# Third attention part: three of its closing products placed elsewhere in the order

## The chip, the cores and the metric

The kernel runs on one core of one Trainium2 chip. The metric is the device time in microseconds (us) of one execution. A core has five engines that each take their own list of instructions strictly in turn: TensorE (PE, matrix products; PEld are its weight loads), VectorE (DVE), ScalarE (ACT), GpSimd (POOL) and SyncE (SP, which here issues DMAs). They wait for one another by semaphores. TensorE writes only to PSUM, eight banks of 128 partitions by 512 fp32 numbers; VectorE and ScalarE carry results from there to SBUF.

## What is computed

Four decoder layers, each with a self-attention, a cross part and a feed-forward part, on x of shape (4, 512, 128), in fp32. The change is in the self-attention of the third layer (in the code `attn2`), causal, with 16 heads of 8 numbers and a learned vector for each clipped distance:

```python
q, k = rotary(shape(x @ w_q.T)), rotary(shape(x @ w_k.T))     # (B, 16, 512, 8)
q = q / sqrt(8)
rel = rel_emb[clip(pos[None, :] - pos[:, None], -32, 32) + 32]
scores = einsum('bhqd,bhkd->bhqk', q, k) + einsum('bhqd,qkd->bhqk', q, rel)
scores = where(causal, scores, NEG_INF)
attn = softmax(scores, axis=-1)
ctx = einsum('bhqk,bhkd->bhqd', attn, v) + einsum('bhqk,qkd->bhqd', attn, rel)
x = x + ctx.transpose(0, 2, 1, 3).reshape(B, L, 128) @ w_o.T
```

## The kernel before, in words

The program is a row of stages; all engines finish one before the next begins. The third attention part is class `Attention2` (line 1356) on top of `Attention` (line 1083), with the distance terms in `Near` (line 1571). It works through batches b of 0 to 3, query tiles of 128 rows (qt, 0 to 3), groups of four heads (g, 0 to 3) and heads j within the group: 4 x 4 x 4 x 4 = 256 units. A unit of query tile qt spans the (qt + 1) x 128 keys up to the diagonal.

What a unit needs, and on which engine:
- *scores*: PE multiplies the masked queries with the keys (`ps<-parts`, one row of 128x128 up to 128x512), DVE reduces the far keys to a minimum (L337) and adds the distance term to the last 160 keys with a running minimum (L343).
- *exp*: ACT takes the exponential from PSUM (L318) and sums it.
- *turned*: four units later PE transposes the weights tile by tile (L311, `ps<-wc_sb,fw_sb 128x128`), and ACT and DVE in turn copy them out of PSUM (L317, L334).
- *inverse*: once in a group DVE takes the reciprocals of four sums (L358); POOL packs the near weights with them (L328) and SP sends them through DRAM to skew them.
- *values*: once in a group PE multiplies the turned weights with the values (L307, `ps<-fw_sb,work` or `ps<-fw_sb`, x8 to x32 in a row).

When the fourth group of a query tile has its values, the *ending* of that tile starts. Its steps, in order:
1. *out*: ACT copies the values' bank (128x512) to SBUF, and DVE spreads the sixteen reciprocals to 512 columns (L334, `fw_sb<-work` or `fw_sb<-fw_sb`, 128x512).
2. *wide*: PE turns that spread table by four products with the identity (L307, `ps<-wc_sb,fw_sb 128x128` x4 in the program; each appears as two in the trace, so x8).
3. *scaled*: DVE multiplies the copied values with it (L321, `fw_sb<-fw_sb,ps`).
4. *output*: PE multiplies with w_o (L307, `ps<-fw_sb,wr_sb 128x128` x4, x8 in the trace).
5. *added*: DVE adds that to x (L321, `xT_sb<-xT_sb,ps`).
6. *weights*, *near values*, *near output* (`Near.ending`, line 1591): PE transposes the skewed near weights (L311, `ps<-wc_sb,work`), DVE copies them (L334, `work<-ps`), PE multiplies with the distance vectors (L307, `ps<-work 128x128` x4), ACT copies, PE multiplies with w_o (L307, `ps<-work,wr_sb`), DVE adds to x.

The order of all this is a list, `self.order`, that `Attention.plan` (line 1118) writes while the kernel is built; every engine then walks the same list and emits what is its own. `step()` is called once after each unit and advances each generator in `bg` to its next `yield`: one is `ending`, another `prepare` (line 1374), which makes the next batch's operands during query tile 3 and places the near product (step *near*) at the start of each query tile. A `yield` is thus one unit's distance. The near product of a tile goes out to DRAM by SP, comes back skewed, and the first scores of that tile wait for it on DVE.

All products other than scores, turned and values share two PSUM banks, ps[6] and ps[7] (`Banks`, line 395): each takes the next bank in turn that is not held, and PE waits in `free` (line 1199) until the bank's last user has been read. *wide* holds its bank until *scaled*, *output* until *added*:

```python
    shared = {"wide": "scaled", "output": "added"}
```

PE's *wide* also waits for the spread table of the DVE, and DVE's *scaled* for *wide*.

Of the kernel before, what the change touches and what calls it, by code (L numbers as in the profile page):

```python
# [1082 lines left out]
class Attention(Stage):  # L1083
# [99 lines left out]
    def ending(self, br):  # L1183
        o = self.order
        self.O.take(br)
        o.append(("out", br))
        yield
        o.append(("wide", br))
        yield
        o.append(("scaled", br))  # L1190
        yield
        yield
        o.append(("output", br))
        yield
        o.append(("added", br))
        if self.rel is not None:
            yield from self.rel.ending(self, br)
# [373 lines left out]
class Near:  # L1571
# [18 lines left out]

    def ending(self, a, br):
        self.PS.take(br)
        for _ in range(7):
            yield
        for what in ("weights", "near values", "near output"):
            a.order.append((what, br))
            yield
            yield

# [2183 lines left out]
```

How the kernel before makes its waits and increments, by code:

```python
    def wait_ge(self, sem, v):  # L301
        if self.e is not None and self.seen.get(sem.name, 0) < v:
            self.e.wait_ge(sem, v)
            self.seen[sem.name] = v
# [282 lines left out]
    def sums_pe(self, e, c):  # L587
        k, t = self.k, self.tag
        e.wait_ge(*k.made_a[t, "square", c])
        e.wait_ge(*k.made_a[t, "deviation", c - 2])
        for i in range(4):
            ins = e.matmul(self.sums[c][:, 64 * i:64 * i + 64], self.sq[:, tile(4 * c + i)], k.cst("mean")[:, 0:64])
        ins.then_inc(*k.summed.up((t, "variance", c)))
# [1 line left out]
    def spread_pe(self, e, c):  # L595
        k, t = self.k, self.tag
        e.wait_ge(*k.made_v[t, "root", c])
        e.wait_ge(*k.made_v[t, "normed", c - 2])
        for i in range(4):
            ins = e.matmul(self.spread[c][:, tile(i)], view(self.r[:, 4 * c + i:4 * c + i + 1], [0, 128]), k.cst("id"))
        ins.then_inc(*k.summed.up((t, "spread", c)))
# [8 lines left out]
    def square_act(self, e, c):  # L610
        k, t = self.k, self.tag
        e.wait_ge(*k.summed[t, "centred", c])
        e.activation(self.sq[:, ch(c)], k.ps[c][:, :], ACT.Square).then_inc(*k.made_a.up((t, "square", c)))
# [1 line left out]
    def root_act(self, e, c, eps):  # L615
        k, t = self.k, self.tag
        e.wait_ge(*k.summed[t, "variance", c])
        e.activation(self.r[:, 4 * c:4 * c + 4], view(self.sums[c], [64, 4]), ACT.Sqrt, bias=k.cst(eps)
                     ).then_inc(*k.made_a.up((t, "deviation", c)))
# [1401 lines left out]
    def turned_pe(self, e, i, X):  # L2021
        e.wait_ge(*self.k.made_a[self.tag, "out", i])
        for c in range(4):
```

## Time and profile before

| | |
|---|---|
| time, median of 3 runs | 3057.36 us (3053.97 to 3064.7) |
| the profiled execution: its time | 3065.82 us |
| the profiled execution: its span | 3064.0 us |
| its mean granted TensorE clock | 0.926 |
| busy over the span | PE 89%, PEld 50%, DVE 56%, ACT 40%, POOL 38% |
| the stage of the change | from 1494 to 1912 us, 418 us |

Times are from one execution taken by the profiler. The granted clock is the share of TensorE's full speed that it was given; matrix products overlap, so that a busy PE is not a PE at its peak. "Idle before" is how long the engine had nothing to do before a row, with the engine that ended the wait.

### The profile page before, as it was taken

The page shows a single profiled execution, that of the slowest core. Times are in us where ns is not written, and L with a number is a line of the kernel's source. Part 1 is how long each engine was busy: PE and PEld are TensorE (multiplying, and loading weights), DVE is VectorE, ACT ScalarE, POOL GpSimd, SP SyncE. Part 2 cuts the span into 40 slices and gives each one's busy share as a digit, 9 for nine tenths or more (in the row PEclk, how much of TensorE's full clock was granted, in tenths as well). Part 3 has the DMA queues.
Part 4 walks back from the last instruction along what each step waited for, and adds up shares of the span by engine and source line. Part 5 has one row for each costly group of instructions (what it writes and reads, how often), then busy time and mean ns, then how long its engine had stood idle before and what let it go on. Part 6 is the DMA issues. An engine that isn't in the chain of part 4 may idle for free. (4 is left out here: it accounts for less than half of the span.)

```text
span 3064.0 us, 39617 instructions
## 1 busy us (share of the span) xinstructions
PE 2734.3 (89%) x15416; PEld 1543.3 (50%) x15416; DVE 1700.6 (56%) x2993; ACT 1223.9 (40%) x2546; POOL 1149.6 (38%) x1045
## 2 busy tenths in 40 slices
PE   6999998899989998978788888999979898998899
PEld 2544454646654444446456656566533333334556
DVE  3444443533337882259587777356466676765623
ACT  1233232333325663133355555366533343432422
POOL 2322220265541100042445443099524443442265
PEclk8999998899997999889799999899989999998999
DMA  2000001011110002046212222211000000001032
GB/s 93 1 1 1 1 1 73 1 56 55 42 53 1 1 1 88 32 101 182 73 54 75 70 58 56 95 42 52 4 1 1 1 1 1 1 1 47 1 132 104
DMA packets 33566, 126.47 MB, mean 41 GB/s; under 512 B 8929, under 2 KB 11746, under 8 KB 27202
## 3 DMA queue, kind: packets, MB, share of 16 engines
q1 hardware_dynamic: 31842, 120.79, 12.1%
q0 software_dynamic: 1536, 3.15, 0.4%
q8 instruction: 121, 1.98, 0.3%
q14 instruction: 67, 0.55, 0.1%
HBM read 106.86 MB, written 17.06 MB: 40 GB/s over the span
## 5 line engine op out<-in xcount | busy, mean ns | idle before, releaser
L307 PE MATMUL ps<-parts 128*128 128x512 f32 (+8 forms) x5544 | 1211.5, 433 | 87.5 <-DVE fw_sb L337 39.7
L307 PEld LDWEIGHTS ps<-parts 128*128 128x128 f32 (+3 forms) x5544 | 673.7, 191 | 610.3 <-issue 291.1
L317 ACT ACTIVATE work<-ps 128x512 f32<-128x512 f32 (+5 forms) x954 | 520.8, 571 | 955.9 <-PE ps L307 862.0
L321 POOL TENSOR_TENSOR work<-work 128x512 f32<-128x512 f32 x380 | 508.3, 1353 | 502.3 <-ACT work L317 298.4
L337 DVE TENSOR_REDUCE fw_sb<-ps 128x2 f32<-128x1024 f32 (+3 forms) x384 | 415.4, 1087 | 274.3 <-PE ps L307 273.3
L307 PE MATMUL ps<-work 128*32 128x256 f32 (+5 forms) x2396 | 365.5, 422 | 8.5 <-DVE work L334 4.9
L307 PE MATMUL ps<-work,fw_sb 128*128 128x512 f32 (+1 forms) x720 | 327.5, 554 | 13.7 <-DVE work L321 8.2
L317 ACT ACTIVATE fw_sb<-ps 128x512 f32<-128x512 f32 (+5 forms) x394 | 204.8, 537 | 308.0 <-PE ps L307 263.9
L321 DVE TENSOR_TENSOR work<-work,ps 128x512 f32<-128x512 f32 (+1 forms) x196 | 121.9, 622 | 283.1 <-POOL work L321 273.0
L311 PE MATMUL ps<-wc_sb,fw_sb 128*128 128x128 f32 x1128 | 209.2, 299 | 36.5 <-DVE work L358 11.7
L307 PEld LDWEIGHTS ps<-work 128*32 128x32 f32 (+2 forms) x2396 | 139.3, 138 | 170.1 <-issue 135.8
L311 PEld LDWEIGHTS ps<-wc_sb,fw_sb 128*128 128x128 f32 x1128 | 133.5, 148 | 104.1 <-issue 28.5
L307 PE MATMUL ps<-fw_sb,wr_sb 64*128 64x512 f32 (+3 forms) x452 | 176.0, 650 | 10.8 <-DVE fw_sb L321 5.3
L318 ACT ACTIVATE fw_sb<-ps,work 128x128 f32<-128x128 f32 (+3 forms) x256 | 135.1, 528 | 118.5 <-DVE work L343 95.2
L321 POOL TENSOR_TENSOR fw_sb<-fw_sb 128x512 f32<-128x512 f32 (+1 forms) x63 | 114.1, 1812 | 166.2 <-ACT fw_sb L317 97.3
L307 PEld LDWEIGHTS ps<-work,fw_sb 128*128 128x128 f32 x720 | 131.6, 197 | 75.6 <-issue 26.0
L317 ACT ACTIVATE work<-ps,wr_sb 128x512 f32<-128x512 f32 (+1 forms) x159 | 108.4, 682 | 129.1 <-PE ps L307 128.9
L334 POOL COPY fw_sb<-work 128x512 f32<-128x512 f32 x32 | 19.6, 611 | 328.7 <-DVE work L358 328.7
L321 POOL TENSOR_TENSOR fw_sb<-fw_sb,work 128x1024 f32<-128x1024 f32 x44 | 103.9, 2360 | 70.4 <-ACT work L317 70.4
L343 DVE CUSTOM_DVE_ANT_0 ps<-ps,work 128x160 f32<-128x160 f32 (+1 forms) x256 | 116.2, 460 | 20.6 <-PE ps L307 10.0
L307 PE MATMUL ps<-fw_sb,work 128*32 128x128 f32 (+3 forms) x1316 | 125.6, 354 | 1.8 <-DVE fw_sb L334 1.6
L328 POOL TENSOR_SCALAR wr_sb<-fw_sb,work 128x160 f32<-128x160 f32 (+1 forms) x176 | 78.1, 527 | 124.5 <-DVE work L358 119.1
(141 smaller groups left out, 3121.9 us busy)
## 6 DMA issues: line engine op xcount, KB each, us to landing
work<-scr_w SPq DMA_DIRECT2D x29, 1024.0 KB, 4.7
work<-scr_places SPq DMA_DIRECT2D x64, 256.0 KB, 4.0
work<-scr_sk SPq DMA_DIRECT2D x64, 128.0 KB, 2.7
scr_sp<-wr_sb SPq DMA_DIRECT2D x64, 128.0 KB, 2.2
fw_sb<-in_f SPq DMA_DIRECT2D x1, 6528.0 KB, 19.3
fw_sb<-in_f SPq DMA_DIRECT2D x1, 5376.0 KB, 15.1
fw_sb<-in_f SPq DMA_DIRECT2D x1, 4608.0 KB, 18.0
work<-scr_w SPq DMA_DIRECT2D x8, 512.0 KB, 5.7
```

What stands on the lines that cost most here:

```text
L307: return self.e.matmul(o, l, r, start=start, stop=stop) if self.e else Unwritten()
L311: return self.e.transpose(o, i, identity[0:n, 0:n]) if self.e else Unwritten()
L317: return self.e.activation(o, i, f, bias=bias, scale=scale)
L318: return self.e.activation(o, i, f, bias=bias, scale=scale, accum_out=accum)
L321: return self.e.tensor_tensor(o, a, b, op) if self.e else Unwritten()
L328: return self.e.tensor_scalar(o, a, s1, s2, op0, op1)
L334: return self.e.tensor_copy(o, i) if self.e else Unwritten()
L337: return self.e.tensor_reduce(o, i, AX.X, op, negate=neg) if self.e else Unwritten()
L343: return self.e.tensor_tensor_reduce(o, a, b, 1.0, low, ALU.add, ALU.min, accum)
```

## The change

```diff
...
         self.O.take(br)
         o.append(("out", br))
-        yield
+        for _ in range(3):
+            yield
         o.append(("wide", br))
         yield
         o.append(("scaled", br))
-        yield
-        yield
+        for _ in range(4):
+            yield
         o.append(("output", br))
         yield
         o.append(("added", br))
...
         self.PS.take(br)
-        for _ in range(7):
-            yield
+        yield
+        yield
         for what in ("weights", "near values", "near output"):
             a.order.append((what, br))
             yield
             yield
+            yield
```

The first two hunks are in `Attention.ending`, the last in `Near.ending`. Counted in calls of `step()` behind *out* (the first comes after the exp of the unit in which *out* stands), the steps of an ending stand before and after at: *wide* 1 and 3, *scaled* 2 and 4, *output* 4 and 8, *added* 5 and 9, *weights* 12 and 11, *near values* 14 and 14, *near output* 16 and 17. No instruction is added or taken away, and the banks are dealt out anew, since they go by the order. `Attention` has no other subclass, so no other stage changes.

PE, batch 0, at the ending of query tile 1, which falls into the second group of tile 2 (`ps<-parts` is a unit's scores, x8 of 32x128 the values, x3 of L311 a unit's transposes, `wc_sb,fw_sb 128x128 x4` is *wide*, `work,wr_sb` *near output* of the tile before). Before:

```order
L307 MATMUL ps<-work,wr_sb 128x128
L307 MATMUL ps<-parts 128x384
L307 MATMUL ps<-fw_sb,work 32x128 x8
L311 MATMUL ps<-wc_sb,fw_sb 128x128 x3
L307 MATMUL ps<-wc_sb,fw_sb 128x128 x4
L307 MATMUL ps<-parts 128x384
L311 MATMUL ps<-wc_sb,fw_sb 128x128 x3
L307 MATMUL ps<-parts 128x384
L311 MATMUL ps<-wc_sb,fw_sb 128x128 x3
```

and after:

```order
L307 MATMUL ps<-parts 128x384
L307 MATMUL ps<-fw_sb,work 32x128 x8
L311 MATMUL ps<-wc_sb,fw_sb 128x128 x3
L307 MATMUL ps<-work,wr_sb 128x128
L307 MATMUL ps<-parts 128x384
L311 MATMUL ps<-wc_sb,fw_sb 128x128 x3
L307 MATMUL ps<-parts 128x384
L311 MATMUL ps<-wc_sb,fw_sb 128x128 x3
L307 MATMUL ps<-wc_sb,fw_sb 128x128 x4
L307 MATMUL ps<-parts 128x384
```

*wide* moved behind the scores and transposes of two more units, and *near output* from ahead of the values to behind the transposes that follow them.

PE, batch 0, at the ending of query tile 2, which falls into the second group of tile 3 (`lnT_sb,wr_sb 128x512` is a product of `prepare`: the first here *turn*, the second *sine*, of the next batch's queries). Before:

```order
L307 MATMUL ps<-work,wr_sb 128x128
L307 MATMUL ps<-lnT_sb,wr_sb 128x512
L307 MATMUL ps<-parts 128x512
L307 MATMUL ps<-fw_sb,work 32x128 x12
L311 MATMUL ps<-wc_sb,fw_sb 128x128 x4
L307 MATMUL ps<-lnT_sb,wr_sb 128x512
L307 MATMUL ps<-wc_sb,fw_sb 128x128 x4
L307 MATMUL ps<-parts 128x512
L311 MATMUL ps<-wc_sb,fw_sb 128x128 x4
```

and after:

```order
L307 MATMUL ps<-lnT_sb,wr_sb 128x512
L307 MATMUL ps<-parts 128x512
L307 MATMUL ps<-fw_sb,work 32x128 x12
L311 MATMUL ps<-wc_sb,fw_sb 128x128 x4
L307 MATMUL ps<-work,wr_sb 128x128
L307 MATMUL ps<-lnT_sb,wr_sb 128x512
L307 MATMUL ps<-parts 128x512
L311 MATMUL ps<-wc_sb,fw_sb 128x128 x4
```

*wide* left this place; *near output* now stands between the two products of `prepare`. By the dealing of banks, *sine* stood in the bank that *near output* had left and *wide* in that of *turn*; now *sine* stands in the bank of *turn*.

PE, in the same tile, from the last products of *value* (`wr_sb,wc_sb`) on (`parts 128x512` are scores and, in front of other scores, *stack*, the next batch's keys; `fw_sb,wr_sb` is *output*). Before:

```order
L307 MATMUL ps<-wr_sb,wc_sb 128x128
L307 MATMUL ps<-parts 128x512
L311 MATMUL ps<-wc_sb,fw_sb 128x128 x4
L307 MATMUL ps<-parts 128x512 x2
L307 MATMUL ps<-fw_sb,wr_sb 128x128 x4
L307 MATMUL ps<-parts 128x512
L307 MATMUL ps<-fw_sb,work 32x128 x16
L311 MATMUL ps<-wc_sb,fw_sb 128x128 x4
L307 MATMUL ps<-parts 128x512 x3
```

and after:

```order
L307 MATMUL ps<-wr_sb,wc_sb 128x128
L307 MATMUL ps<-wc_sb,fw_sb 128x128 x4
L307 MATMUL ps<-parts 128x512
L311 MATMUL ps<-wc_sb,fw_sb 128x128 x4
L307 MATMUL ps<-parts 128x512 x3
L307 MATMUL ps<-fw_sb,work 32x128 x16
L311 MATMUL ps<-wc_sb,fw_sb 128x128 x4
L307 MATMUL ps<-parts 128x512 x3
```

*wide* now follows *value* directly, ahead of the next scores, and *output* has left this place: it stands four units later, one unit ahead of the next batch's near product. The second *stack* product used the bank of the first; now it uses the bank of *wide*.

## Rows read from the trace of the kernel before

**Rows 1.** Stage window: us, busy PE, PEld, DVE, ACT, POOL (instructions), clock, DMA.
```profile
1494.00:1912.00 418.00, 345.13 (x2842) 247.05 (x2841) 314.37 (x1042) 218.87 (x689) 198.92 (x349) 0.91 0.23 64
```

**Rows 2.** Waits in the stage: who waited for whom, us in all, times, longest.
```profile
ACT fw_sb L318 <- DVE work L343: 95.2, 134, 2.9
...
DVE work L337 <- PE ps L307: 28.8, 18, 2.7
```

**Rows 3.** Timeline behind query tile 1 of batch 1: start, us, [idle before].
```profile
1651.56 0.64 PE L307 MATMUL ps<-fw_sb 128*32 128x128 f32 x16
...
1653.53 0.53 DVE L334 COPY fw_sb<-fw_sb 128x512 f32<-128x512 f32 x1
...
1654.12 2.08 PE L307 MATMUL ps<-wc_sb,fw_sb 128*128 128x128 f32 x8 [1.44 <-DVE fw_sb L334]
...
1656.55 0.39 DVE L337 TENSOR_REDUCE work<-ps 128x1 f32<-128x224 f32 x1 [2.03 <-PE ps L307]
```

**Rows 4.** Groups of L337 in the stage: busy, mean ns, idle before.
```profile
L337 DVE TENSOR_REDUCE work<-ps 128x1 f32<-128x96 f32 x64 | 15.7, 245 | 6.1 <-PE ps L307 6.1
...
L337 DVE TENSOR_REDUCE work<-ps 128x1 f32<-128x224 f32 x64 | 24.2, 379 | 7.0 <-PE ps L307 7.0
...
L337 DVE TENSOR_REDUCE work<-ps 128x1 f32<-128x352 f32 x64 | 33.0, 515 | 15.8 <-PE ps L307 15.7
```

**Rows 5.** Timeline of VectorE behind query tile 2 of batch 3.
```profile
1884.61 0.53 DVE L337 TENSOR_REDUCE work<-ps 128x1 f32<-128x352 f32 x1 [0.88 <-PE ps L307]
```

**Rows 6.** Timeline in query tile 2 of batch 1, behind its first groups.
```profile
1658.12 1.16 PE L307 MATMUL ps<-fw_sb,wr_sb 128*128 128x128 f32 x8
...
1661.50 0.44 PE L307 MATMUL ps<-parts 128*128 128x384 f32 x1 [0.23 <-ACT fw_sb L318]
...
1662.91 0.39 DVE L337 TENSOR_REDUCE work<-ps 128x1 f32<-128x224 f32 x1
```

**Rows 7.** Timeline in query tile 3 of batch 1.
```profile
1681.84 1.16 PE L307 MATMUL ps<-wc_sb,fw_sb 128*128 128x128 f32 x8 [1.59 <-DVE work L331]
...
1683.27 0.53 DVE L337 TENSOR_REDUCE work<-ps 128x1 f32<-128x352 f32 x1 [1.49 <-PE ps L307]
...
1684.98 0.49 PE L307 MATMUL ps<-wr_sb,lnT_sb 128*128 128x128 f32 x2 [0.64 <-DVE work L331]
...
1690.96 1.91 PE L307 MATMUL ps<-fw_sb,wr_sb 128*128 128x128 f32 x8
...
1693.33 0.52 DVE L337 TENSOR_REDUCE work<-ps 128x1 f32<-128x352 f32 x1 [2.73 <-PE ps L307]
...
1696.93 0.97 PE L307 MATMUL ps<-parts 128*128 128x512 f32 x3 [1.38 <-DVE parts L334]
...
1697.93 0.53 DVE L337 TENSOR_REDUCE work<-ps 128x1 f32<-128x352 f32 x1 [0.87 <-PE ps L307]
```

**Rows 8.** Timeline from the near product of batch 1 to its first scores.
```profile
1602.17 0.69 DVE L334 COPY work<-ps 128x512 f32<-128x512 f32 x1 [0.17 <-PE ps L307]
...
1602.89 1.70 SPq L372 DMA_DIRECT2D scr_sk<-work  x4
...
1610.76 0.38 DVE L343 CUSTOM_DVE_ANT_0 ps<-ps,work 128x128 f32<-128x128 f32 x1 [2.27 <-DMA work<-scr_sk]
```

**Rows 9.** Timeline in query tile 0 of batch 1.
```profile
1616.97 1.06 PE L307 MATMUL ps<-wc_sb,fw_sb 128*128 128x128 f32 x8
...
1618.12 0.38 DVE L343 CUSTOM_DVE_ANT_0 ps<-ps,work 128x128 f32<-128x128 f32 x1 [0.67 <-PE ps L307]
```

**Rows 10.** Timeline at the stage's end.
```profile
1904.93 1.70 SPq L372 DMA_DIRECT2D work<-scr_sp  x4
...
1908.44 0.66 PE L311 MATMUL ps<-wc_sb,work 128*128 128x128 f32 x4 [0.58 <-DVE xT_sb L321]
```

**Rows 11.** Windows behind one ending, and in query tile 3, of batch 1.
```profile
1652.00:1656.00 4.00, 2.56 (x20) 2.19 (x12) 2.45 (x9) 1.72 (x5) 2.95 (x5) 0.71 0.43 112
...
1688.00:1692.00 4.00, 4.00 (x15) 3.40 (x15) 1.95 (x5) 1.34 (x4) 1.81 (x4) 0.50 0.00 0
```

## The prediction

> **What bounds the kernel now.** The order is written out by hand, so I read the stage alone. First its window: PE is busy for 345.1 of 418 us and DVE for 314.4, at a granted clock of 0.91 [rows 1]. Neither is full, so waits decide, and I went to them. Two stand out: ACT waits for DVE's running minimum, 95.2 us in 134 waits, each short, and DVE waits for PE ahead of its reduction L337, 28.8 us in only 18 waits [rows 2]. The first says that in the ordinary run of units DVE leads and the others follow. The second is time in which this leader stands, in few large pieces, and that is what a change of the order can give back.
>
> Where the pieces are, the timeline tells. Behind query tile 1 of batch 1, PE has done the values and the transposes, and the next thing in its list is *wide*. DVE spreads the reciprocals only at 1653.53, so PE stands for 1.44 us, then takes 2.08 us for *wide*, and the scores behind it come late: DVE's next reduction starts after 2.03 us of idle [rows 3]. The groups by form sort the 28.8 us by query tile, since the width of L337 does: 6.1 us in tile 1, 7.0 in tile 2, 15.7 in tile 3 [rows 4]. In tiles 1 and 2 the waits are one for each of the four batches, all behind *wide*. In tile 3 they are four waits behind *wide* (1.49 us at the batches 0 to 2, as in the first DVE row of rows 7, and 0.88 at batch 3 [rows 5]), and six others, 15.7 - 3 x 1.49 - 0.88 = 10.3 us, all in batches 0 to 2, where the next batch is prepared.
>
> **The change part by part.** No instruction comes or goes; only waits can change.
>
> *Wide* two units later, in tiles 1 and 2, and in tile 3 of batch 3 (nine places). PE goes on with the next scores, while DVE spreads the reciprocals and turns to its next unit; when PE reaches *wide*, the table is two units old. The stall goes whole: 6.1 + 7.0 + 0.9 = 14.0 us. What is late next? *Wide* itself still takes 1.1 us of PE, ahead of a unit's scores. The cover is the pair of scores that PE has in hand. In rows 6 the scores product at 1661.50 had waited 0.23 us for ACT and is read by DVE at 1662.91, so it is finished about 1.0 us early (1662.91 less 1661.94). A block of 1.16 us ahead of it eats first the wait and then 0.9 of this 1.0. The trace has the case: *output*, 1.16 us at 1658.12, stands in the same kind of place, and no wait of DVE follows it [rows 6]. I take nothing for *wide* and for *output* at the new places. Bounds: 14.0 us gained, and from that down by up to 1.16 us at each of nine *wides* (10.4) if the cover is missing.
>
> *Wide* in tile 3 of batches 0 to 2 (three places). Here PE's stall of 1.59 us ended with a DVE instruction of L331, not with the spread table [rows 7]: *wide* stood in the bank of *turn*, and had to wait until DVE had read it. After the change *sine* stands in that bank, right in front of the same scores, and waits for the same read. It is a product of 1.0 us like *wide*. So the 3 x 1.49 = 4.5 us stay. Bounds: nothing to 4.5 us gained.
>
> The Trainium skill, "Perfetto Trace Analysis", section "Matmuls", says that independent groups of products should rotate through the PSUM banks, so that the read-out of one overlaps the next. By that rule the new *turn* and *sine* in one bank speak against the change, and the three stalls of 1.49 us stay. The trace agrees as far as it goes: the 1.59 us are a wait for a bank's reader [rows 7].
>
> The rest of tile 3, batches 0 to 2. (a) *Wide* now follows *value*. *Value* itself no longer waits 0.64 us for its bank [rows 7], *wide* adds 1.06: the next scores come 0.4 us later. (b) *Output* leaves its place at 1690.96, where it held PE until 1692.52 (the next row starts there), 1.56 us, and DVE stood 2.73 [rows 7]: 1.6 us gained; *scaled*, 0.68 us of DVE, falls into the idle time that is left there. (c) The second *stack* has another bank than the first, so that PE's 1.38 and DVE's 0.87 us [rows 7] go: 0.9 gained. (d) *Output* now stands one unit ahead of the near product of the next batch. DVE copies it at 1602.17 after waiting 0.17 for PE, and then 8.6 us of DRAM and back pass until the first scores of the next batch, which wait 2.27 us for that transfer [rows 8]. Whatever delays the copy, delays the batch: 1.0 us lost for an *output* at full clock. Sum: -0.4 + 1.6 + 0.9 - 1.0 = 1.1, I take 1.0 us for each batch, 3.0 in all. Bounds: all six waits gone, 10.3 us gained; and, with both products at the 1.9 us that *output* took here [rows 7] and nothing but (b) and (c) returned, 0.64 - 1.9 + 1.6 + 0.9 - 1.9 = -0.7 a batch, 2.0 us lost.
>
> The endings of tile 3, which fall into tile 0 of the next batch (three). *Wide* follows PE's own work without a wait there, and DVE stands 0.67 us after it [rows 9]: in these short units PE leads. The same 1.06 us come two units later. Nothing; bounds one wait each, 3 x 0.67 = 2.0 us either way.
>
> *Weights* one unit earlier, *near output* one later: the transposes wait for the transfer of the packed weights, which at the stage's end is issued at 1904.93 and waited for no longer than 1908.44 [rows 10], 3.5 us; and PE stands behind no DMA there: its wait of 0.58 us is for DVE. Nothing. SP's list keeps its order. In the tail *weights* of the last tile start 0.04 us after DVE's addition but also just when the transfer is in, so a shorter chain has nothing behind it: nothing, to 0.5 either way.
>
> Sum: 14.0 + 0 + 3.0 = 17.0 us. Against the profiled execution, 3065.8, whose span is 3064.0, that makes 3048.8. That execution lies 8.5 us above the median of the runs, 3057.36, and above their highest, 3064.7; I take the same microseconds off the median: 3057.4 - 17.0 = 3040.4 us.
>
> **The rivals.**
>
> A. *The clock comes back too.* In the 4 us around the stall of rows 3 the granted clock was 0.71, and where tile 3's *output* ran it was 0.50, the lower level of 1.2 GHz, with PE busy all of the 4 us and DVE 1.95 of them [rows 11]. Take the stalls away and PE may keep 2.4 GHz; then also the six waits of tile 3 and the stall in front of *sine* shrink. For it: the 1.91 us of *output* against 1.16 elsewhere. Against it: the stall of 1.59 us that precedes the low stretch stays. All 28.8 us go: 3057.4 - 28.8 = 3028.6. The skill's page "TensorE: Matmul & The Clock Gate", section "A second HAM failure mode: psum-queue depth-cycling", describes short idles between groups of products that make the clock swing between its levels; by it, this is how it goes.
>
> B. *The products show again.* *Wide* at the end of a group comes when DVE has just waited for the reciprocals' sums and the cover is thin; DVE waits 0.6 us at each of the twelve places in tiles 1 to 3 (1.06 of *wide* and 0.44 of scores, less a cover of 0.9), and tile 3 goes by its lower bound. For it: the cover of rows 6 is just long enough. Against: *output* there. 14.0 - 7.2 - 2.0 = 4.8 us gained: 3052.6, which a measurement of this kernel can't tell from no change.
>
> C. *Slower: PE falls to the lower clock for longer.* A mean of 0.91 [rows 1], if all of it is time at half speed, is 0.18 x 418 = 75 us at the lower level. In such a stretch DVE stands for 2.05 of 4 us [rows 11], half of the time. Of the stage's 103.6 us of DVE idle (418 - 314.4 [rows 1]) that is 38, and the other 66 spread over 343 us, 0.19 of the time. Each microsecond more at the lower level thus costs 0.32. If *value* with *wide*, and *output* with the values behind it, leave gaps in which the clock falls, and the low time doubles, 75 x 0.32 = 24 us are lost: 3057.4 - 14.0 + 24 = 3067.4. It decides from some 72 more us at 1.2 GHz ((14.0 + 9.2) / 0.32). Against it: the change removes idle time of PE.
>
> **How the numbers follow.** My forecast 0.61, with a range of its own of 3034 to 3047 (17.0 us, from 23 down to 10); A 0.14, B 0.16, C 0.09. This kernel's measurement can tell some 0.3%, 9.2 us, from no change: faster is below 3048.2, slower above 3066.5. Faster: 0.59 of the forecast and A, 0.73. Slower: C, 0.08. The same: B and the rest, 0.19. The range must reach from near A to past B: 3030 to 3055, leaving out C and half of A.
>
> **What would show it.** Right: the wait of L337 for PE falls from 28.8 to some 12 us, and its parts for 96 and 224 columns to nearly nothing; the four products of *wide* have no idle before them in tiles 1 and 2; in tile 3 *sine* of the queries has 1.1 us or more of idle, ended by DVE L331, and the 1.49 us of DVE behind it stay; no 1.38 us in front of the second *stack*. The copy of the near product waits about 1 us for PE, and the first scores of batches 1 to 3 still wait for the transfer. Wrong: a stage that is not 10 us shorter than 418, DVE waits of 0.5 us or more behind the new *wide* or *output* (B), or a stage clock under 0.88 (C) or over 0.95 (A).

## The result, and the profile after

| | before | after |
|---|---|---|
| median of five runs each, side by side | 3053.97 us (3052.38 to 3064.7) | 3036.34 us (3034.98 to 3042.4) |
| ratio, with its 95% interval | | 0.9939 (0.9919 to 0.9959) |
| the same kernel in a later session, 29 and 12 runs | 3052.04 us (3039.46 to 3069.63) | 3043.46 us (3032.54 to 3055.61) |
| ratio there | | 0.9959 (0.9938 to 0.9980) |
| span and granted clock of the profiled execution | 3064.0 us, 0.926 | 3033.4 us, 0.935 |

By the ratios the change gains 18.6 us (12.5 to 24.7) in the first session and 12.5 us (6 to 19) in the second; by the medians it is 17.6 and 8.6. 17.0 were predicted.

The window of the stage, cut at the same points of the work as in [rows 1] (columns as there), and two of its parts, query tile 3 of batch 1 and of batch 2:

```profile
1486.80:1892.10 405.30, 332.22 (x2842) 239.70 (x2840) 314.91 (x1042) 217.75 (x689) 198.77 (x349) 0.93 0.23 66
1656.39:1691.48 35.09, 27.60 (x248) 20.21 (x247) 29.83 (x76) 18.06 (x44) 12.71 (x22) 1.00 0.13 31
1752.32:1793.56 41.24, 33.70 (x248) 24.80 (x247) 30.03 (x77) 17.84 (x44) 12.68 (x22) 0.83 0.10 26
```

12.7 us are gone from 418.00. VectorE works as long as before (314.91 us), so what went is its idle time. The last two rows are the same instructions in the same order, and one takes 6 us more than the other, at a granted clock of 0.83 against 1.00. That must be kept in mind for all of tile 3.

The wait behind the 28.8 us of [rows 2], and the groups of L337 that answer to [rows 4]:

```profile
DVE work L337 <- PE ps L307: 10.3, 12, 1.7
DVE parts L334 <- PE ps L307: 9.7, 6, 2.2
```

```profile
L337 DVE TENSOR_REDUCE work<-ps 128x1 f32<-128x352 f32 x64 | 33.0, 516 | 9.3 <-PE ps L307 9.2
...
L337 DVE TENSOR_REDUCE work<-ps 128x1 f32<-128x224 f32 x64 | 24.3, 379 | 0.0
...
L337 DVE TENSOR_REDUCE work<-ps 128x1 f32<-128x96 f32 x64 | 15.8, 247 | 1.1 <-PE ps L307 1.1
```

The 7.0 us of tile 2 are 0.0, the 6.1 of tile 1 are 1.1 (all in batch 1, at a clock of 0.91), the 15.7 of tile 3 are 9.2. The second wait was 4.9 us in three waits before. What is new is VectorE's copy of the *stack* products at the turn from one batch to the next, 4.7 us in three waits.

A part of what went in tile 2 belongs to the clock. Tile 2 of batches 0 and 1 of the kernel before, of batch 1 of the changed kernel, and of batch 0 of e10 (a later run, with *wide* at its new place; columns as in [rows 1]):

```profile
1544.56:1566.97 22.41, 19.11 (x178) 13.43 (x176) 19.43 (x66) 14.23 (x43) 11.20 (x20) 1.00 0.26 72
1645.82:1669.34 23.52, 19.88 (x175) 14.42 (x173) 19.49 (x66) 14.12 (x43) 11.19 (x20) 0.93 0.25 69
...
1634.86:1656.39 21.53, 18.30 (x178) 13.16 (x177) 19.52 (x66) 14.10 (x43) 11.18 (x20) 1.00 0.28 75
...
1539.44:1560.84 21.40, 19.16 (x178) 14.25 (x177) 19.38 (x67) 14.32 (x43) 11.19 (x20) 0.92 0.28 75
```

At full clock the tile went from 22.41 to 21.53 us, 0.9 less. At the old place a low clock costs 1.0 us more, since *wide* itself then takes 2.0 to 2.1 us in place of 1.16 while VectorE stands for it; three of the four tiles 2 of the profile before were such. At the new place a low clock costs nothing in this tile (21.40 at 0.92); in tile 1 of batch 1, where it met *wide* too, it still cost 1.1 us.

The ending of query tile 1 of batch 1, answering to [rows 3]:

```profile
1642.37 0.66 DVE L334 COPY fw_sb<-fw_sb 128x512 f32<-128x512 f32 x1
...
1643.61 0.38 DVE L337 TENSOR_REDUCE work<-ps 128x1 f32<-128x224 f32 x1
...
1643.93 1.06 PE L307 MATMUL ps<-wc_sb,fw_sb 128*128 128x128 f32 x8
...
1644.43 0.38 DVE L337 TENSOR_REDUCE work<-ps 128x1 f32<-128x224 f32 x1
```

The table is spread 0.9 us before *wide* begins, TensorE takes *wide* without idle time, and VectorE's reductions on either side don't wait.

Query tile 3 of batch 1, answering to [rows 7], and the same place in batch 2 from its *value* on:

```profile
1668.36 0.68 DVE L331 SCALAR_TENSOR_TENSOR work<-ps,wr_sb 128x512 f32<-128x512 f32 x1
1669.09 1.13 PE L307 MATMUL ps<-lnT_sb,wr_sb 128*128 128x512 f32 x2 [2.99 <-DVE work L331]
...
1670.48 0.52 DVE L337 TENSOR_REDUCE work<-ps 128x1 f32<-128x352 f32 x1 [1.45 <-PE ps L307]
...
1773.89 2.08 PE L307 MATMUL ps<-wc_sb,fw_sb 128*128 128x128 f32 x8
1774.00 0.69 DVE L334 COPY fw_sb<-ps 128x512 f32<-128x512 f32 x1 [3.18 <-PE ps L307]
...
1776.43 0.53 DVE L337 TENSOR_REDUCE work<-ps 128x1 f32<-128x352 f32 x1 [1.74 <-PE ps L307]
```

*Sine* waits for the reader of *turn*, 2.99 us, and VectorE then stands 1.45. In batch 2 TensorE fell to half clock behind that, *wide* took 2.08 us, and VectorE stood 3.18 and 1.74 us more, which batch 1 did not.

The turn from batch 0 to batch 1, answering to [rows 8]:

```profile
1590.73 0.69 DVE L334 COPY work<-ps 128x512 f32<-128x512 f32 x1 [0.17 <-PE ps L307]
...
1595.85 3.13 PE L307 MATMUL ps<-parts 128*128 128x512 f32 x6 [2.90 <-DVE parts L334]
...
1597.96 0.69 DVE L334 CAST parts<-ps 128x512 fp32r<-128x512 f32 x1 [2.17 <-PE ps L307]
...
1600.10 0.38 DVE L343 CUSTOM_DVE_ANT_0 ps<-ps,work 128x128 f32<-128x128 f32 x1 [1.45 <-PE ps L307]
...
1602.02 0.69 DVE L334 COPY work<-ps 128x512 f32<-128x512 f32 x1 [1.49 <-PE ps L307]
```

The near copy waits 0.17 us, as before. The first scores of the batch wait no longer for the transfer but for TensorE, which is in the chain of stack products and their copies. TensorE stood 2.90 us in front of the second of them and was at half clock from 1.2 to 4.6 us behind the tile's start, while it made this one and the next two.

### The profile page after: what moved, and what is told of

Same layout as the page of the kernel before. It is cut to its first block and busy times, and to the rows that moved or that the text cites. A ratio compares the mean times of both kernels' runs of the same rounds, so it can differ in the third digit from the quotient of the medians.

```text
span 3033.4 us, 39609 instructions
## 1 busy us (share of the span) xinstructions
PE 2703.9 (89%) x15416; PEld 1528.3 (50%) x15416; DVE 1700.5 (56%) x2993; ACT 1221.4 (40%) x2546; POOL 1149.9 (38%) x1045
## 5 line engine op out<-in xcount | busy, mean ns | idle before, releaser
L337 DVE TENSOR_REDUCE fw_sb<-ps 128x2 f32<-128x1024 f32 (+3 forms) x384 | 415.3, 1087 | 269.3 <-PE ps L307 268.3
L311 PE MATMUL ps<-wc_sb,fw_sb 128*128 128x128 f32 x1128 | 207.8, 297 | 48.3 <-DVE fw_sb L334 15.4
L311 PEld LDWEIGHTS ps<-wc_sb,fw_sb 128*128 128x128 f32 x1128 | 132.5, 146 | 116.4 <-issue 30.3
L307 PE MATMUL ps<-fw_sb,wr_sb 64*128 64x512 f32 (+3 forms) x452 | 169.4, 626 | 10.7 <-DVE fw_sb L321 4.9
L321 DVE TENSOR_TENSOR parts<-work,parts 128x512 fp32r<-128x512 f32 x68 | 80.7, 1191 | 77.4 <-ACT parts L317 77.4
## 6 DMA issues: line engine op xcount, KB each, us to landing
fw_sb<-in_f SPq DMA_DIRECT2D x1, 4608.0 KB, 17.6
```

Of the source, the lines that this page charges most:

```text
L307: return self.e.matmul(o, l, r, start=start, stop=stop) if self.e else Unwritten()
L311: return self.e.transpose(o, i, identity[0:n, 0:n]) if self.e else Unwritten()
L321: return self.e.tensor_tensor(o, a, b, op) if self.e else Unwritten()
L337: return self.e.tensor_reduce(o, i, AX.X, op, negate=neg) if self.e else Unwritten()
```

## The experiments

Each kernel's stage is split here by query tile, from one tile's last reciprocals (L358) to the next one's: us in tile 1, in tile 2 (four each), in tile 3 of batches 0 to 2 with the granted clock of each, and in tile 0 of batches 1 to 3. The total has the two remaining tiles too, tile 0 of batch 0 and tile 3 of batch 3. Times and ratios are against the kernel before of the same session; three sessions, in the order of the numbers 1 to 4, 5 to 8, 9 to 12.

| kernel | tile 1 | tile 2 | tile 3, b0-2 | clock there | tile 0, b1-3 | total | median us | ratio (95%) |
|---|---|---|---|---|---|---|---|---|
| before | 80.8 | 92.7 | 114.6 | .91 .91 .95 | 60.5 | 385.7 | 3053.4, 3052.0, 3049.7 | 1 |
| after | 74.9 | 86.1 | 113.0 | .95 1.00 .83 | 62.5 | 372.8 | 3036.3 | .9939 |
| e5 after again | 74.7 | 86.1 | 111.8 | 1.00 .91 .91 | 62.7 | 371.6 | 3043.5 | .9959 (.9938-.9980) |
| e1 wide only | 75.1 | 85.5 | 117.1 | .91 .87 .87 | 62.2 | 375.9 | 3041.2 | .9973 (.9955-.9991) |
| e2 near only | 78.5 | 91.5 | 115.0 | .87 1.00 .96 | 63.7 | 385.7 | 3053.3 | 1.0004 (.9985-1.0022) |
| e3 output only | 79.7 | 90.6 | 112.5 | .91 .91 .95 | 62.5 | 382.2 | 3047.5 | .9997 (.9977-1.0016) |
| e4 near output 16 | 75.3 | 85.5 | 101.2 | 1.00 .90 1.00 | 63.2 | 361.2 | 3029.4 | .9932 (.9907-.9957) |
| e6 after, wide x2 | 76.1 | 86.1 | 114.4 | .91 .95 .95 | 65.3 | 378.1 | 3045.1 | .9977 (.9953-1.0000) |
| e7 before, wide x2 | 85.6 | 94.7 | 112.5 | .95 1.00 .96 | 65.2 | 396.4 | 3068.0 | 1.0034 (1.0016-1.0052) |
| e8 e4 + stack earlier | 73.3 | 85.4 | 98.7 | 1.00 1.00 1.00 | 58.0 | 351.4 | 3019.1 | .9878 (.9847-.9908) |
| e9 after, idle filled | 73.8 | 86.1 | 114.3 | .96 .96 .96 | 63.0 | 372.6 | 3040.4 | .9966 (.9946-.9985) |
| e10 e4 + stack by two | 73.9 | 85.4 | 102.8 | 1.00 1.00 1.00 | 63.7 | 361.9 | 3031.6 | .9922 (.9897-.9946) |
| e11 after, wide x4 | 83.0 | 93.0 | 127.4 | .92 .88 .84 | 70.9 | 412.0 | 3077.2 | 1.0082 (1.0050-1.0114) |
| e12 before, stack earlier | 83.0 | 90.7 | 113.0 | .91 .95 .95 | 66.4 | 390.1 | 3056.9 | 1.0012 (.9994-1.0030) |

**e1, e2, e3: one part at a time.** Steps behind *out* of *wide*, *scaled*, *output*, *added*, *weights*, *near values*, *near output*:

```diff
-before  1 2 4 5 12 14 16
+e1      3 4 6 7 12 14 16
+e2      1 2 4 5 11 14 17
+e3      1 2 8 9 12 14 16
```

> Only wide (and scaled behind it) moves, from 1 unit behind out to 3; output goes from 4 to 6 to stay behind scaled, weights, near values and near output stay at 12, 14 and 16. Theory (the gain is the removed wait of TensorE for the spread table): the stalls in tiles 1 and 2 go (12.5 us by the trace of the changed kernel), and in tile 3 of batches 0 to 2 sine of the queries stands in the bank that near output left one unit earlier, not in that of turn, so the three stalls of 1.45 us go as well: 14 to 20 us below the kernel before, thus level with the changed kernel or up to 4 us better. L337's wait for TensorE: 5 to 9 us. Rival (the gain comes from the three products together, by a higher clock): at most 8 us below before, and the stage's clock no higher than before.

> Only the near steps move: weights 12 to 11, near output 16 to 17; wide and output stay. Theory: nothing in tiles 1 and 2 (the 12.5 us of stalls stay); in tile 3 of batches 0 to 2 the bank of turn goes to sine instead of wide, so the 1.49 us only change place; in tile 0 of batches 1 and 2 the near product's copy loses about 1.0 us each by the new bank order. Time 0 to 3 us above the kernel before. Rival (the near steps carry a part of the gain): 3 us or more below.

> Only output moves, from 4 to 8 units behind out. Theory: tiles 1 and 2 as before (output is covered at both places), tile 3 of batches 0 to 2 gains 1.6 us each where output left the stack products and loses up to 1.0 at the near product: 0 to 3 us below the kernel before; L337's wait for TensorE 22 to 28 us. Rival (output's place sets the clock of tile 3): tile 3 of batches 0 to 2 gains 3 us each, 9 us in all.

Moving *wide* alone brings the whole gain of tiles 1 and 2 (13.0 us of it in the profile), and the times of e2 and e3 can't be told from before. How large the gain is depends on the clock of the profile that it is measured against: with *wide* at its old place tiles 1 and 2 took 173.5 us in before and 173.7 in e12, but 170.0 in e2 and 170.3 in e3, and with *wide* alone moved 160.5. So it lies between 9.5 and 13 us. *Output* at 8 (e3) takes 0.7 us off each tile 3, at the same clocks as before.

But e1 missed its expectation: 8 us by the ratio (3 to 14) and 12 by the medians, not 14 to 20, and L337 waited 17.4 us for TensorE, not 5 to 9. Tile 3 lost 2.5 us, although *sine* no longer waited for *turn*. TensorE in tile 3 of batch 0 of e1, and VectorE behind it:

```profile
1581.54 2.07 PE L307 MATMUL ps<-fw_sb,wr_sb 128*128 128x128 f32 x8 [1.57 <-ACT parts L317]
...
1584.08 0.52 DVE L337 TENSOR_REDUCE work<-ps 128x1 f32<-128x352 f32 x1 [3.89 <-PE ps L307]
```

At 6, *output* stands in the bank of the second *stack* and waits for ScalarE to have copied it, 1.6 us in each of the three batches. At 8 it does not. So e1 exchanges one stall for another. That it is worse than the changed kernel is not shown: its tile 3 of batch 0 takes 38.15 us at a clock of 0.91, and e5 has 38.31 at the same clock; its two longer tiles had 0.87, and the ratios of e1, after and e5 overlap.

**e4: *near output* back at 16.** The changed kernel with the last step one unit earlier, 3 4 8 9 11 14 16.

> The changed kernel with near output back at 16 units, so that it again stands ahead of turn of the queries and sine gets the bank that near output left. Theory (the idle before sine is the reader of its bank): the idle of TensorE before sine of the queries (2.99 us in batch 2) and the 1.45 us of VectorE behind it go in three places, and the near product of tile 1 again gets the bank of near values, which gives back the 1.0 us in tile 0 of batches 1 and 2: 4 to 6 us below the changed kernel, 22 to 25 below the kernel before. Rival (sine waits because VectorE is late with everything there, or the stall moves on to value, whose bank is now that of turn): within 1.5 us of the changed kernel.

Tile 3 of batch 0, where *sine* now has the bank that *near output* left:

```profile
1565.03 1.12 PE L307 MATMUL ps<-lnT_sb,wr_sb 128*128 128x512 f32 x2 [0.29 <-DVE xT_sb L321]
...
1566.43 0.68 DVE L334 COPY fw_sb<-ps 128x512 f32<-128x512 f32 x1
1567.03 0.67 DVE L331 SCALAR_TENSOR_TENSOR work<-ps,wr_sb 128x512 f32<-128x512 f32 x1
1567.63 0.51 DVE L337 TENSOR_REDUCE work<-ps 128x1 f32<-128x352 f32 x1
```

2.99 us of TensorE have become 0.29, and VectorE doesn't stand. The tile takes 32.72 us at a clock of 1.00, where the changed kernel takes 35.09 and 35.11 at 1.00; at about 0.91 it is 35.79 against 38.31. So the other deal of banks is worth 2.4 us a tile, not the 1.45 of the stall's one row: the wait of 0.57 us behind *value* and *wide* is gone too. And the clock stayed at 1.00 in two of three.

```profile
1555.25:1587.97 32.72, 28.02 (x248) 20.13 (x247) 29.50 (x76) 18.09 (x44) 12.78 (x22) 1.00 0.13 33
```

Tile 3 lost 10.6 to 11.8 us against the two profiles of the changed kernel, twice the 4 to 6 us that were expected of the whole kernel; tile 0 gave nothing back (63.2), so that part of the expectation was wrong. The times don't resolve e4 from the changed kernel: 0.9932 against 0.9939 and 0.9959, with intervals that overlap.

**e5: the changed kernel again.**

> The changed kernel once more, for a second profile and for its spread. Theory (query tile 3 of batches 0 to 2 is the same in its first 18 us, and then the granted clock falls or does not, by no order of its own): each of these three tiles takes some 35 us where the clock stays at 1.00 and 36.5 to 41 where it falls, in other batches than in the first profile; tiles 1 and 2 repeat within 0.3 us; time 3032 to 3045. Rival (the clock in a tile belongs to the order): 36.7, 35.1 and 41.2 us for batches 0, 1 and 2 again.

The low clock came in other batches: 35.1, 38.3 and 38.4 us, where the first profile had 36.7, 35.1 and 41.2. Tile 2 repeated to 0.02 us, tile 1 of batches 0 and 1 differed by 0.6 and 0.8, at another clock.

```profile
1561.72:1596.83 35.11, 27.58 (x248) 20.18 (x247) 29.87 (x77) 18.09 (x44) 12.76 (x22) 1.00 0.11 31
1657.99:1696.30 38.31, 30.77 (x248) 22.53 (x247) 30.05 (x77) 17.86 (x44) 12.74 (x22) 0.91 0.11 29
```

**e6, e7, e11: how much work the places cover.**

```diff
-                for c in range(4):
-                    ins = e.matmul(X[:, tile(c)], self.wide[:, tile(c)], k.cst("id"))
+                for c in range(8):
+                    ins = e.matmul(X[:, tile(c % 4)], self.wide[:, tile(c % 4)], k.cst("id"))
```

> The changed kernel with the four products of wide issued twice into the same bank: 1.06 us more of TensorE at each of 16 places. Theory (the new place is covered by about 1.0 us in tiles 1 and 2, so one wide is hidden and a second is not): 0.5 to 1.0 us at each of the eight places in tiles 1 and 2, 0.3 to 1.0 in tile 3 and 0: 6 to 14 us above the changed kernel. Rival 1 (there is ample cover): under 3 us in tiles 1 and 2 together. Rival 2 (the first wide already shows): the full 1.06 us at each, 17 us.

> The kernel before with the products of wide issued twice. Theory (TensorE stands for the spread table and VectorE then stands for TensorE, so every bit of work added there shows): 1.06 us or more at each of the eight places in tiles 1 and 2, and in tile 3: 12 to 18 us above the kernel before. Rival (wide was hidden there too, and only the table's lateness counted): under 6 us.

> The changed kernel with the four products of wide issued four times: 3.2 us more of TensorE at each of 16 places. With two times, tiles 1 and 2 took no more than 0.1 us each more at a clock of 1.00. Theory (the cover at the new place is about 2 us, since TensorE's idle time in the two units around counts beside the scores finished early): 1 to 2 us at each of the eight places in tiles 1 and 2, 8 to 16 us there. Rival (there is slack for 3 us and more): under 4 us in these eight tiles. In tile 3 and tile 0 about 2.5 us more each in both.

At the new place a second *wide* costs next to nothing in tiles 1 and 2, as the first rival of e6 had it and not its theory: -0.1 us in all of tile 2, and 1.3 in tile 1 against e5, 1.8 of it in batch 3 alone, where the clock was 0.92 and not 1.00. At the old place it costs 6.8 us in these eight tiles, 0.85 of its 1.06 each (tile 2 at full clock goes from 22.41 to 23.27); of the whole kernel it costs 10 us by the ratio (5 to 16) and 16 by the medians, where 12 to 18 were expected. Four times *wide*, 3.2 us more at each place, costs 8.3 in tile 1 and 6.9 in tile 2, 1.9 a place, within the 8 to 16 us expected; in tile 3 it costs 15.6 us, twice what was expected, at lower clocks than in e5, and in tile 0 8.2. The cover in tiles 1 and 2, the first *wide* included, is thus 4.2 - 1.9 = 2.3 us (an estimate from these runs), where 0.9 to 1.0 were read from the trace. VectorE behind a doubled *wide* (TensorE has it from 1651.69 to 1653.64) in e6:

```profile
1652.88 0.55 DVE L334 COPY fw_sb<-ps 128x384 f32<-128x384 f32 x1
1653.76 0.18 DVE L358 RECIPROCAL work<-work 128x4 f32<-128x4 f32 x1 [0.33 <-ACT fw_sb L318]
1653.86 0.39 DVE L337 TENSOR_REDUCE work<-ps 128x1 f32<-128x224 f32 x1
```

Between the two reductions it has a copy and the reciprocals, and waits there for ScalarE; the scores that *wide* delays come just in time. In tiles 3 and 0, without such room, e6 pays.

**e9: the idle time filled.** In *near output* of the tiles that fall into tile 3, ahead of its own wait:

```diff
+        if qt == 1 and b < 3:
+            for _ in range(4):
+                e.matmul(X[:, :], k.wt(2, "wk"), k.lnT[:, ch(b)])
```

> The changed kernel, with four products of 128x512 (some 1.8 us of TensorE, their result is overwritten) put ahead of near output in query tile 3 of batches 0 to 2. They fall into the 2.99 us in which TensorE stands in front of sine, of which 1.1 us remain; VectorE's 1.45 us and its waits stay as they are. Theory (the granted clock falls because TensorE has just stood idle for about 3 us): the clock of tile 3 stays near 1.00 in batches 0 to 2 and each of them takes 35 to 36 us, where the changed kernel had 35.1, 35.1, 36.7, 38.3, 38.4 and 41.2: 3 to 8 us below the changed kernel. Rival (the dip comes from something else, or more work makes the clock fall more): tile 3 at a clock of 0.83 to 0.95 in at least two of three, and no time below the changed kernel.

The four products took 3.60 us, not 1.8, so *near output* came late and VectorE stood 1.33 us more for it: the run prices the filling badly. TensorE then stood 1.0 us in front of *sine*, not 3.0. The clock still tells something. In the 5 us behind the start of *sine* it had fallen in 8 of the 12 profiled tiles with the whole stall (after, e5, e6, e11) and in none of the 9 without (e4, e8, e10), and here it stayed at 1.00 in all three. With the other profiles it is 10 of 15 (e2 has the stall too) against 1 of 24 (before, e1, e3, e7, e12 don't have it there). The limit of 5 us is arbitrary, and near it the counts are soft: one tile of e4, one of e1 and two of e6 fell 5.2 to 5.5 us behind that start. In e9 it fell in all three tiles at 6.2 to 6.3 us, where *value* ends and *wide* runs, with TensorE busy from *sine* on, and the tile had 0.96 in the mean. So neither expectation was met: the counts speak for a part of the idle time in the early fall, and what makes the later one is open.

**e8, e10, e12: the turn of a batch.** In `prepare`, behind the near product of the next batch; e8 and e12 take away one yield (e8 on top of e4, e12 on the kernel before), e10 both on top of e4:

```diff
             self.rel.plan(self, b, 0)
             yield
-            yield
             self.Q.take(b)
```

> Near output at 16 as in the earlier run, and the first stack product of the next batch's queries one unit earlier (one yield less behind the near product), so that the last unit of a batch holds one step less of the chain stack, copy, stack between TensorE and VectorE. Theory (at the turn of a batch this chain ends last, no longer the near transfer): 1 to 1.5 us less at each of three turns, 3 to 4.5 us below the version with near output at 16, 3022 to 3028. Rival (the near transfer, 8.6 us from its copy to the scores, is hardly earlier than the chain): 0 to 1 us less.

> As the version with near output at 16 and the first stack of the queries one unit earlier, but two units earlier, right behind the near product. Theory (the chain stack, copy, stack bounds the turn of a batch): another 0.5 to 1.3 us at each of three turns, until the near transfer ends last: 1 to 4 us below that version. Rival (the near transfer already ends last, and stack 0 now stands in the near product's own bank and ahead of its copy's turn in the order): 0 to 3 us above it.

> The kernel before, with only the first stack product of the next batch's queries one unit earlier. Theory (before, the first scores of a batch waited for the near transfer, 2.27 us, so that the chain of stacks was hidden): 0 to 1.5 us below the kernel before in all. Rival (the chain of stacks ended last before as well): 3.5 to 5 us below it.

e8 is the best kernel found: 1.2% below before by the ratio, and 24.4 us below the changed kernel of its session. Its profile has 5.2 us less than e4 in tile 0 (58.0 against 63.2), where 3 to 4.5 were expected of the whole kernel; at a like clock (0.91 and 0.92) it is 1.3 to 1.4 us a turn. It has the full clock in all three tiles 3, and L337 hardly waits any more:

```profile
DVE work L337 <- PE ps L307: 1.4, 3, 0.5
```

One step more (e10) loses it again, more than either of its expectations had: tile 3 takes 34.3 us in place of 32.9, at full clock in both, and the near product of the next tile is then copied only after VectorE has stood for 3.60 us in tile 0 of batch 1, and the clock there is 0.84 in all three.

```profile
1603.23 0.69 DVE L334 COPY work<-ps 128x512 f32<-128x512 f32 x1 [3.60 <-PE ps L307]
```

On the kernel before (e12) the same edit gives nothing, at most 1.8 us by the ratio, which excludes the rival's 3.5 to 5; in the profile tile 0 is 5.9 us longer: *weights* stand in another bank, the first scores wait 3.13 us for TensorE, and the clock is 0.85 to 0.89 there. What an edit at the turn is worth thus depends on the order that it is made in.

## Why the prediction was right, by its steps

- *Wide* in tiles 1 and 2 and at the end: 14.0 us predicted. Measured 5.9 + 6.6 + 0.8 = 13.3 in the first profile, 6.1 + 6.6 + 0.8 = 13.4 in the second. Right in place, and e1 shows that *wide* alone carries it. The size has some luck in it: both the 14.0 and the 13.3 are measured against one profile, in which the stalled *wide* took 1.59 to 2.08 us in six of the eight tiles 1 and 2, where it takes 1.16 at full clock. In tile 2, 3.5 of the 6.6 us are the stall at full clock, and 3.1 are what the low clock added to it. Against e2 and e3, with *wide* at its old place as well, tiles 1 and 2 gained 9 us.
- The cover of the new place: right that it holds, too small by more than half (2.3 us in place of 1.0). It was read off one product finished early; the copy, the reciprocals and their wait that VectorE also has in these units were not counted. Rival B hung on the cover being thin: e6 shows that in tiles 1 and 2 twice the work would hardly have shown.
- The stall moves from *wide* to *sine* in tile 3 of batches 0 to 2: the row is there in all three batches, 1.45 us where 1.49 was said. That nothing is gained there was right. Its price was not: e4 shows 2.4 us a tile for the bank that *sine* stands in.
- The rest of tile 3: 3.0 us predicted with no part for the clock. All of this tile, batches 0 to 2, gained 1.7 and 2.8 us in the two profiles. That these are near the sum is partly luck, for the tile's duration goes from 35.1 to 41.2 us with the clock. At like clocks the gain is smaller: 38.71 us before against 38.31 and 38.38 at 0.91, 37.20 against 36.65 at 0.95, thus 0.3 to 0.6 a tile where 1.0 was said. The waits of (b) and (c), 2.73 and 0.87 us, are gone as predicted, so the sum of the terms is about twice too large; which of them is mis-sized, these runs don't tell. Term (d) as put is refuted: the near copy waits 0.17 us, not 1.0.
- The endings in tile 0: nothing predicted, 2.0 and 2.2 us lost, at the edge of the bounds. The failed step is that the first scores of a batch wait for the near transfer; before, they did so in batches 1 and 2 and waited for TensorE in batch 3, where its clock was low. With the new order of the banks the second *stack* of the queries waits for the copy of the first (before, it had the near product's bank), *weights* stand ahead of it, and the chain of TensorE and VectorE ends last. e8 shortens this chain and gets 5.2 us. How much of the 2.0 is the chain and how much the clock is open: before, the two turns at full clock took 19.8 us and the one at 0.88 took 21.0, and the changed kernel has 20.8 to 21.0 at 0.92 in all six.
- Tail and *near output*: nothing predicted; from the last reciprocals to the last addition 12.9 us before and after.
- The sum: 17.0 predicted, 12.9 and 14.1 us in the stage's two profiles, 18.6 and 12.5 in the two sessions. The profiled spans differ by 30.6 us, and 17.7 of that lie outside the stage, where nothing was changed: the profiled execution of before was among its slowest, as the prediction had allowed for by counting from the median.
- Rival A (the clock comes back) came in part: all eight profiled tiles 2 of the changed kernel (after, e5) had the full clock, where three of four before had 0.93. It did not come in the stage as a whole: 0.91 became 0.93, and L337 still waits 10.3 us, nearly all in tile 3. That is what the change leaves undone: with *sine* free and the chain shorter, e8 has that wait at 1.4 us, and the time that rival A named and more. Rival C did not come, though its mechanism is real in single tiles (41.24 us at 0.83).

## What to carry to other kernels

Where products share two PSUM banks in the order of issue, moving one step deals the banks anew for all that follow: write down for each step of the new order whose bank it gets and when that is read, since a stall that leaves one product can reappear at another (*sine* here, *output* in e1). A product that waits for a slower engine's table is best issued a few units later, and how much cover it has there is found by issuing it twice and four times. A stall that holds TensorE's own work is longer at half clock: read it in several tiles, and compare tiles at like clocks. Change one step of such an order at a time, then look at the combination: here *near output* put back at 16 took 2.4 us more off each tile 3, and the first *stack* of the queries one unit earlier 1.3 to 1.4 us more off each turn at a like clock.

## What the hardware showed that was not expected

The same instructions in the same order ran tile 3 at a granted clock of 1.00, 0.95, 0.91 or 0.83, from execution to execution and batch to batch, 35.1 to 41.2 us. Where TensorE had stood for 3 us in front of *sine*, the clock was down within the next 5 us in 10 of 15 profiled tiles; without that stand in 1 of 24. The Trainium skill, "TensorE: Matmul & The Clock Gate", section "A second HAM failure mode: psum-queue depth-cycling", tells of short idles between groups of products that make the clock swing; this comparison agrees in its direction, but the later fall in e9, behind 6 us without idle time, is not explained by it. A single tile can so differ by 6 us between two executions, and one profile of a kernel says little on an edit of that size in tile 3. And a product of 128x512 in fp32 took 0.90 us in a row of four (3.60 us), since each appears as two records: the estimate of 1.8 us had counted a record for a product.
